# Shared gate rows and weight parts made by GpSimd transfers, in a ViT tower kernel with routed experts

## The chip, the cores and the metric

One core of a Trainium2 chip runs the whole program. The metric is the device time of one execution in microseconds; lower is better. In the rows, PE is TensorE's matmuls, PEld its weight loads, DVE VectorE, ACT ScalarE, POOL GpSimd, SP SyncE.

## The reference, cut to what matters

32 images of 96x96 pixels are cut into 36 patches each; with a class token there are T = 37 tokens an image and C = 192 channels.

```python
h   = einsum('bnk,ok->bno', patches, W)              # tok; the class token is put ahead
h   = x0 = LN(h); k, v, r = x0 @ Wk, x0 @ Wv, x0 @ Wr
x1  = x0 + (sigmoid(r) * bi_wkv(decay, first, k, v)) @ Wo      # two scans over tokens
h   = (h + x1) + sigmoid(LN(x1) @ Wr_f) * (relu(LN(x1) @ Wk_f)**2 @ Wv_f)
c   = routing of LN(h): 16 experts in 4 groups, the best 4 of the best 2 groups, weights * 2.5
hs  = silu(x @ sWg + sbg) * (x @ sWu + sbu)                    # shared expert, 192 wide
he  = silu(einsum('th,ehi->tei', x, gWg) + gbg) * (... gWu + gbu)   # 16 experts, 96 wide
out = h + hs @ sWd + sbd + einsum('te,teh->th', c, he @ gWd + gbd)
```

(LN, the gains and the residual order are shortened here; the shape of the work is what matters.)

## The kernel before, in words

The 1184 tokens are cut into four groups of 6, 10, 10 and 6 images (222, 370, 370 and 222 columns). Each group g goes through a front F{g} (patches, first norm, k/v/r, scans, Wo), a middle M{g} (second norm, `up0..5` and `mix0..5`, third norm, router logits and the routing on VectorE), and 14 expert units: `G{g}:g{n}` and `v{n}` are the gate and value matmuls of unit n on TensorE, `Y{g}:e{n}` its silu on ScalarE, `S{g}:s{n}` the product on VectorE, `X{g}:x{n}` the multiplication by the token's gate, `D{g}:d{n}` the down matmul. Units 0 and 1 are the shared expert; units 2 to 13 are the 16 experts' 1536 inner rows in 12 chunks of 128 rows. As an expert has 96 rows, a chunk covers parts of two experts, and three chunks (a period) cover four.

Each engine takes its steps in the order of a list written out by hand or by a planner (`PE_ORDER`, `ACT_ORDER`, `DVE_ORDER`, `POOL_ORDER`; L1248 to L1311). `advance` (L293) walks it; nothing is reordered at run time, so a step that waits holds up all behind it on its engine. `W:` and `L:` are steps on weights, `H:` are spins: matmuls of a constant tile that keep TensorE at work early on (L1018).

**Weights.** The matmuls that need float32 accuracy use two parts of each weight, `hi` (rounded to fp32r) and `lo` (the rest). `PIECES` (L60) are loaded by SyncE through a ring of four buffers `raw` that lies in the `gates` tile (L126 to L128). For each piece ScalarE makes `hi` by a copy (L400). For pieces before `egu0` (k, v, r, rf, up0, up1, router, sgu) VectorE subtracts to make `lo` (L610); for the six `egu` pieces TensorE does it with identity matmuls into the PSUM tile PA (L1014, L1015), in twelve halves, and ScalarE copies each half out (L409). `split` (L108) is the wait for a piece's `lo`.

**Gates.** Once group g is routed, ScalarE copies the 16 experts' gate rows out (`C{g}:cT`, L586), SyncE stores them to `c_rows` in DRAM (L329) and reads them back, each row broadcast over the partitions of its expert, by 24 transfers a group (L338): six `SPANS` for each of four periods. For g > 0 each period waits until the group before has used its gates (L335). `patches(3)`, the pixels for F3, is issued by SyncE behind the 24 transfers of group 0 (L368, L369); the stores of a finished group behind those of a later one.

**The stretch that the change moves most.** VectorE does F0's scans and products (L699 to L771), whose end is `F0:z`, then F1's, and between them the middle of group 0. GpSimd takes the inverse roots of the variances (L391), twelve in all. TensorE's front of group 1 (`F1:tr1a` on) is followed by `F1:sub0..2` (subtractions in PSUM, L1118), M0 and then the units of group 0 from `G0:g0`, which need `stack3`, VectorE's `M0:tr3a` and `M0:tr3b` (L678).

## Time and profile before

| what | value |
|---|---|
| runs before | 258.48 us median of 3 (258.15 to 259.61) |
| the profiled execution | 259.53 us, of which the span of its records is 257.6 us |
| busy in the span | PE 245.2, DVE 191.2, ACT 151.5, POOL 17.1 us |
| chain that ended last | PE 74%, DVE 9%, ACT 9%, issue 3%, DMA 2% |
| HBM read | 16.22 MB, mean 67 GB/s |

The profile is one execution. Each engine's records are listed with what ended the idle time before them; the chain is the work that ended last, followed back from the end. A busy PE includes matmuls whose end is modelled, and matmuls overlap, so the distance between the starts of two pieces of work is the better measure of their cost.

### The profile page before, as it was taken

The numbers are of one execution on the slowest core, as the hardware profiler recorded it, in microseconds if no ns is written. First come the engines' busy times: TensorE is split into PE (matmuls) and PEld (weight loads), VectorE is DVE, ScalarE is ACT, GpSimd is POOL, SyncE is SP. The second block draws the span as 40 slices with busy tenths as digits, with TensorE's granted clock in tenths as the row PEclk, the third lists the DMA queues.
The fourth block names the chain that finished last, engine by engine and source line by source line (L and its number), as shares of the span: only waits on it lengthen the run. The fifth ranks groups of instructions, "written<-read, shape, count | busy, mean of one in ns | idle before, by whom it ended". The sixth has DMA issues, their size and how long they took to land.

```text
span 257.6 us, 4492 instructions
## 1 busy us (share of the span) xinstructions
PE 245.2 (95%) x1508; PEld 222.6 (86%) x1508; DVE 191.2 (74%) x491; ACT 151.5 (59%) x312; POOL 17.1 (7%) x26
## 2 busy tenths in 40 slices
...
GB/s 154 211 191 286 212 186 119 0 3 0 0 0 6 84 111 57 0 3 0 1 3 121 187 76 4 1 3 0 54 163 158 29 3 0 1 23 109 102 29 26
DMA packets 13015, 17.49 MB, mean 68 GB/s; under 512 B 2336, under 2 KB 11074, under 8 KB 12866
## 3 DMA queue, kind: packets, MB, share of 16 engines
...
q8 instruction: 12, 0.20, 0.3%
q10 hardware_dynamic: 272, 0.11, 0.2%
...
HBM read 16.22 MB, written 0.99 MB: 67 GB/s over the span
## 4 chain that ended last, share of the span: by engine, by line
PE 74%; DVE 9%; ACT 9%; issue 3%; DMA 2%; POOL 0%; SPq 0%; DVEq 0%; POOLq 0%; ACTq 0%
PE PG L964 18%; PE PA L984 17%; PE PG L966 11%; PE PF L984 7%; PE PQ L964 4%; PE PQ L966 3%; PE PX L1001 2%; PE PF L1001 2%; ACT norm L417 2%; DMA w_tok<-in_w_tok 2%; PE PF L974 1%; PE PG L1119 1%; PE PG L1118 1%; DVE K L763 1%; PE PF L991 1%
## 5 line engine op out<-in xcount | busy, mean ns | idle before, releaser
L575 ACT ACTIVATE act<-PG,columns 128x222 f32<-128x222 f32 (+3 forms) x56 | 28.4, 507 | 59.0 <-PE PG L966 45.9
L964 PE MATMUL PG<-stack,hi_egu 128*128 128x222 f32 (+1 forms) x288 | 62.2, 324 | 0.0
L913 DVE SCALAR_TENSOR_TENSOR hid<-PG,columns,act 128x222 f32<-128x222 f32 (+1 forms) x52 | 27.3, 524 | 29.3 <-PE PG L966 26.7
L984 PE MATMUL PA<-w_ed,hid 128*124 128x192 f32 (+1 forms) x240 | 46.1, 327 | 0.6 <-DVE hid L922 0.5
L964 PEld LDWEIGHTS PG<-stack,hi_egu 128*128 128x128 f32 x288 | 45.7, 191 | 0.9 <-DVE hid L913 0.4
L966 PE MATMUL PG<-stack,lo_egu 128*128 128x222 f32 (+1 forms) x192 | 42.8, 304 | 0.0
L984 PEld LDWEIGHTS PA<-w_ed,hid 128*124 128x124 f32 (+1 forms) x240 | 38.6, 183 | 1.3 <-issue 1.3
L966 PEld LDWEIGHTS PG<-stack,lo_egu 128*128 128x128 f32 x192 | 31.8, 191 | 0.0
L391 POOL TENSOR_TENSOR rstd<-var,minus_half 112x2 f32<-112x2 f32 (+3 forms) x12 | 13.8, 1146 | 191.7 <-DVE var L657 191.7
L922 DVE TENSOR_TENSOR hid<-hid,gates 128x222 f32<-128x222 f32 (+1 forms) x48 | 21.9, 461 | 1.6 <-DMA gates<-c_rows 0.7
L984 PE MATMUL PF<-w_down,mix_hid 128*124 128x192 f32 (+1 forms) x120 | 22.8, 326 | 0.0
L984 PEld LDWEIGHTS PF<-w_down,mix_hid 128*124 128x124 f32 (+1 forms) x120 | 19.5, 183 | 0.3 <-issue 0.2
L740 DVE TENSOR_TENSOR_SCAN S<-E,S 128x333 f32<-128x333 f32 (+1 forms) x16 | 16.2, 1062 | 0.2
L964 PE MATMUL PQ<-stack,hi_up 128*128 128x222 f32 (+1 forms) x72 | 15.3, 320 | 0.0
L541 ACT ACTIVATE relu<-PQ 128x222 f32<-128x222 f32 (+1 forms) x24 | 9.9, 414 | 5.6 <-PE PQ L966 5.3
L1014 PE MATMUL PA<-gates,columns 128*128 128x512 f32 x24 | 12.5, 602 | 0.7 <-ACT lo_egu L409 0.7
L763 DVE RECIPROCAL K<-K 128x222 f32<-128x222 f32 (+3 forms) x8 | 12.2, 1531 | 0.1
L417 ACT ACTIVATE norm<-h,shift,rstd 124x192 f32<-124x192 f32 (+1 forms) x20 | 9.6, 537 | 3.9 <-DVE shift L664 3.8
L964 PEld LDWEIGHTS PQ<-stack,hi_up 128*128 128x128 f32 x72 | 11.3, 191 | 0.5 <-issue 0.5
L1021 PE MATMUL PQ<-still 128*128 128x256 f32 x36 | 10.5, 451 | 1.1 <-POOL still L385 1.1
L547 ACT ACTIVATE mix_hid<-relu 128x222 f32<-128x222 f32 (+1 forms) x24 | 10.8, 451 | 0.8
L966 PE MATMUL PQ<-stack,lo_up 128*128 128x222 f32 (+1 forms) x48 | 10.7, 304 | 0.0
...
## 6 DMA issues: line engine op xcount, KB each, us to landing
gates<-in_w_egu SPq DMA_DIRECT2D x6, 512.0 KB, 4.9
...
```

Source lines behind the costliest of these rows:

```text
L391: nc.gpsimd.tensor_tensor(small[n]["rstd"][0:G.tp, 0:cols, 0:G.tiles], small[n]["var"][0:G.tp, 0:cols, 0:G.tiles], minus_half[0:G.tp, 0:co ...
L417: last = nc.scalar.activation(norm[n][0:G.tp, t, :], x[0:G.tp, t, :], ACT.Identity, bias=small[n]["shift"][0:G.tp, col, t:t + 1], scale=sm ...
L547: nc.scalar.activation(mix_hid[:, m % 2, 0:G.n], relu[:, 0:G.n], ACT.Square).then_inc(act_square, 1)
L575: nc.scalar.activation(act[128 - gate:128, n % 2, 0:G.n], PG[0:gate, gate_bank(n), 0:G.n], ACT.Silu, bias=bias).then_inc(act_silu, 1)
L740: step(V_.tensor_tensor_scan(run(x, d), run(E1[:, d * WK:d * WK + wk], d), run(x, d), 0.0, ALU.mult, ALU.add))
L763: step(V_.reciprocal(K[:, s], K[:, s]))
L913: V_.scalar_tensor_tensor(out, PG[part, 1, 0:G.n], bias, act[part, i, 0:G.n], ALU.add, ALU.mult).then_inc(mul_done, 1)
L922: V_.tensor_tensor(out, out, gates[:, n - SCH, 0:G.n], ALU.mult).then_inc(hid_ready, 1)
L964: mm(out, w_hi[:, slot, cols], x[:, p, 0:G.n], start=(p == 0), stop=False, skip_group_check=True)
L966: last = mm(out, w_lo[:, p, cols], x[:, p, 0:G.n], start=False, stop=(p == 1), skip_group_check=True)
L984: last = mm(tile_out(P, G, t), src[:, G.ts[t]:G.ts[t] + G.tp], w, start=start and t != 1, stop=stop, skip_group_check=True)
L1014: mm(PA[:, s, 0:cols], ident32, raw[n % RING][:, s * cols:(s + 1) * cols], start=True, stop=False)
```

## The change

Two things are changed, and all four order lists are new.

Gates: the experts' rows are laid out anew (`_beside`): a period's 384 rows are arranged so that each of its three chunks has 32 rows of each of four experts. One gate tile of 128 partitions then serves three chunks. A group takes 4 transfers, each reading 4 rows of `c_rows` and repeating each over 32 partitions. There are two sets of gate tiles in turn, in the tile `ring`, and the wait is for the group two before.

Weights: rf, up0, up1, sgu and egu0 to egu5 no longer go through the ring. GpSimd issues a converting transfer from DRAM for `hi` (`W:`), ScalarE writes its negative to `lo` (`L:` in ACT_ORDER), and GpSimd issues a second transfer from DRAM which adds the weight to it (`L:` in POOL_ORDER). ScalarE's `hi` copies of these pieces, VectorE's four subtractions, TensorE's identity matmuls and ScalarE's copies of their results are gone. PA is free in that stretch, so the subtractions `F0:sub` and `F1:sub` go there, and a few waits follow.

```diff
     yield from ((m, 128, 2, cols, True) for m, cols in (("k", 256), ("v", 128), ("r", 256)))
-    yield ("rf", 128, 2, C, True)
-    yield from ((f"up{i}", 128, 2, HID // 2, True) for i in range(2))
     yield ("router", 128, 2, EXPERTS, True)
-    yield ("sgu", 128, 2, 2 * C, True)
-    yield from ((f"egu{i}", 128, 2, 512, True) for i in range(ECH // 2))
+
+
+def _cast_pieces():
+
+    yield ("rf", C)
+    yield from ((f"up{i}", HID // 2) for i in range(2))
+    yield ("sgu", 2 * C)
+    yield from ((f"egu{i}", 512) for i in range(ECH // 2))
...
-        gates = sb("gates", [128, ECH, N])
-        flat_gates = gates[:, :, :].rearrange("p c n -> p (c n)")
-        raw = [flat_gates[:, i * RING_COLS:(i + 1) * RING_COLS] for i in range(RING)]
+        ring = sb("ring", [128, RING * RING_COLS])
+        raw = [ring[:, i * RING_COLS:(i + 1) * RING_COLS] for i in range(RING)]
+        gates = [[ring[:, (i * PERIODS + j) * N:(i * PERIODS + j + 1) * N] for j in range(PERIODS)] for i in range(2)]
...
-            return PG[:, :, :].rearrange("p b c -> p (b c)") if g else (PQ, PX)[i % 2]
+            return PA[:, :, :].rearrange("p b c -> p (b c)") if g else PA[:, i % 2, :]
```

SyncE's part, then GpSimd's, ScalarE's and TensorE's:

```diff
                 if g == 0:
-                    split(sp, len(PIECES))
+                    sp.wait_ge(lo_done, len(PIECES))
                 for j in range(PERIODS):
-                    if g:
-                        sp.wait_ge(hid_ready, at(hid_ready, g - 1, 3 * (j + 1)))
-                    for chunk, a, b, e in SPANS:
-                        expert = 4 * j + e
-                        sp.dma_start(gates[a:b, 3 * j + chunk, 0:n],
-                                     A["c_rows"][g, expert:expert + 1, 0:n].broadcast_to([b - a, n])).then_inc(gates_in[j], 16)
+                    if g >= 2:
+                        sp.wait_ge(hid_ready, at(hid_ready, g - 2, 3 * (j + 1)))
+                    rows = A["c_rows"][g, BESIDE * j:BESIDE * (j + 1), None, 0:n].broadcast_to([BESIDE, 128 // BESIDE, n])
+                    sp.dma_start(gates[g % 2][j][:, 0:n], rows).then_inc(gates_in[j], 16)
...
             piece(5)
             patches(1)
-            for n in range(6, 8):
-                piece(n)
             unsplit("down")
-            for n in range(8, 10):
-                piece(n)
             unsplit("sd")
-            for n in range(10, 13):
-                piece(n)
             unsplit("ed")
-            for n in range(13, len(PIECES)):
-                piece(n)
             patches(2)
             gates_across(0)
             patches(3)
```

```diff
-            for n, g in POOL_ORDER:
-                root(n, g, 2 if n == 1 else 1)
+            def pool_roots(pool, g):
+                for n in (1, 2, 3):
+                    root(n, g, 2 if n == 1 else 1)
+                    yield f"root{n}"
+
+            def pool_casts(pool):
+                for name, _ in CAST:
+                    nc.gpsimd.dma_start(hi[name][:, :, :], A[f"w_{name}"]).then_inc(cast_in[name], 16)
+                    yield name
+
+            def pool_lows(pool):
+                for n, (name, _) in enumerate(CAST):
+                    pool.wait_ge(act_minus, n + 1)
+                    nc.gpsimd.dma_start(lo[name][:, :, :], A[f"w_{name}"], accum_op=ALU.add).then_inc(low_in[name], 16)
+                    yield name
+
+            tracks = tracks_of(pool, pool_casts, R=pool_roots)
+            advance({**tracks, "L": pool_lows(pool)}, POOL_ORDER)
```

```diff
+        def act_minus_parts(act_e):
+
+            for name, _ in CAST:
+                act_e.wait_ge(cast_in[name], 16)
+                nc.scalar.activation(lo[name][:, :, :], hi[name][:, :, :].bitcast(F32), ACT.Copy, scale=-1.0).then_inc(act_minus, 1)
+                yield name
...
-            split(pe, PIECE_AT[name] + 1)
+            if name in low_in:
+                pe.wait_ge(low_in[name], 16)
+            else:
+                pe.wait_ge(lo_done, PIECE_AT[name] + 1)
...
-
-        def pe_low_parts(pe):
-
-            pe.wait_ge(consts_done, 1)
-            for i, (name, _, slots, cols, _) in enumerate(PIECES[FIRST_EGU:]):
-                n = FIRST_EGU + i
-                for s in range(slots):
-                    k = 2 * i + s
-                    if k >= 2:
-                        pe.wait_ge(act_low, k - 1)
-                    pe.wait_ge(hi_done, n + 1)
-                    mm(PA[:, s, 0:cols], ident32, raw[n % RING][:, s * cols:(s + 1) * cols], start=True, stop=False)
-                    mm(PA[:, s, 0:cols], minus_ident[:, :], hi[name][:, s, :], start=False, stop=True).then_inc(pe_low, 1)
-                    yield f"{name}{'ab'[s]}"
```

The lists up to the first units of group 0 (the rest is rearranged in the same manner):

```diff
-POOL_ORDER = [(1, 0), (1, 1), (2, 0), (1, 2), (3, 0), (2, 1), (1, 3), (3, 1), (2, 2), (3, 2), (2, 3), (3, 3)]
+POOL_ORDER = _order(
+    "R0:root1 R1:root1 W:rf W:up0 W:up1 W:sgu W:egu0 W:egu1 W:egu2 L:rf L:up0 R0:root2 L:up1 L:sgu R2:root1 W:egu3 W:egu4",
+    "W:egu5 L:egu0 L:egu1 L:egu2 R0:root3 R1:root2 L:egu3 L:egu4 L:egu5 R3:root1 R1:root3 R2:root2 R2:root3 R3:root2",
+    "R3:root3",
+)
 PE_ORDER = _order(
-    "H:early0 H:early1 H:early2 H:early3 F0:tok0 H:early4 H:early5 H:tok H:stats0 H:stats1 H:aggr H:var H:rstd F0:tr1a",
-    "F0:tr1b F1:tok0 F1:tok1 F0:k F0:kt F0:v F0:rt F0:r H:scan0 H:scan1 H:sb0 H:sb1 H:e1 H:edge F0:sub0 F0:sub1 F0:sub2",
-    "W:egu0a W:egu0b W:egu1a F1:tr1a F1:tr1b W:egu1b W:egu2a F0:o0 F1:k F1:kt F1:v W:egu2b F1:rt F1:r M0:tr2 F2:tok0",
-    "W:egu3a F2:tok1 F1:sub0 M0:rf M0:up0 F1:sub1 M0:up1 M0:mix0 F1:sub2 M0:up2 M0:mix1 M0:up3 M0:mix2 M0:up4 M0:mix3",
-    "M0:up5 W:egu3b M0:mix4 M0:mix5 F2:tr1a W:egu4a W:egu4b F2:tr1b W:egu5a W:egu5b M0:tr3 F1:o0 M0:logits F1:o1 G0:g0",
-    "G0:g1 F2:k G0:v1 G0:g2 F2:kt G0:v2 G0:g3 F2:v D0:cT G0:v3 G0:g4 F2:rt D0:d1 M1:tr2 F2:r G0:v4 G0:g5 D0:d0 M1:rf M1:up0",
-    "D0:d2 D0:d3 M1:up1 M1:mix0 G0:v5 G0:g6 M1:up2 M1:mix1 D0:d4 M1:up3 M1:mix2 F3:tok0 G0:v6 M1:up4 M1:mix3 G0:g7 G0:v7",
...
+    "H:early0 H:early1 H:early2 H:early3 H:early4 F0:tok0 H:early5 H:tok H:stats0 H:stats1 H:aggr H:var F0:tr1a F0:tr1b",
+    "H:rstd F1:tok0 F1:tok1 F0:k F0:kt F0:v F0:rt F0:r H:scan0 H:scan1 H:sb0 H:sb1 H:e1 F0:sub0 F0:sub1 F0:sub2 F1:tr1a",
+    "F1:tr1b H:edge F1:k F1:kt F0:o0 F1:v F1:rt F1:r F2:tok0 F1:sub0 F2:tok1 F1:sub1 M0:tr2 F1:sub2 M0:rf M0:up0 M0:up1",
+    "M0:mix0 M0:up2 M0:mix1 F2:tr1a M0:up3 M0:mix2 M0:up4 M0:mix3 M0:up5 M0:mix4 F2:tr1b M0:mix5 F1:o0 F1:o1 M0:tr3 F2:k",
+    "G0:g0 M0:logits G0:g1 F2:kt G0:v1 G0:g2 F2:v G0:v2 G0:g3 F2:rt D0:cT D0:d1 G0:v3 G0:g4 M1:tr2 F2:r G0:v4 G0:g5 D0:d0",
+    "M1:rf M1:up0 D0:d2 F3:tok0 G0:v5 M1:up1 M1:mix0 D0:d3 G0:g6 M1:up2 M1:mix1 G0:v6 D0:d4 M1:up3 M1:mix2 G0:g7 D0:d5",
...
 )
 ACT_ORDER = _order(
-    "W:cls W:mask W:k W:v F0:tok0 W:r F0:ln1 Z0:x0 F0:tr1a F0:tr1b W:rf W:up0 W:up1 F0:k F0:kt F0:vt F0:kf F0:v F0:rt",
-    "W:router F1:tok0 F1:tok1 F0:r F0:exps F0:expe W:sgu W:egu0 F0:w0 F0:w1 F0:w2 W:egu1 W:egu2 L:egu0a F0:wr F1:ln1",
-    "L:egu0b L:egu1a F1:tr1a F1:tr1b L:egu1b L:egu2a W:egu3 F1:k F1:kt F1:vt F1:kf F1:v M0:ln2 F1:rt Z1:x0 F1:r F1:exps",
-    "F2:tok0 M0:tr2 F2:tok1 F1:expe F1:w0 L:egu2b M0:rf M0:mix0 W:egu4 F1:w1 M0:mix1 W:egu5 F1:w2 M0:mix2 L:egu3a M0:mix3",
-    "M0:mix4 F1:wr M0:mix5 F2:ln1 L:egu3b F2:tr1a L:egu4a L:egu4b F2:tr1b M0:ln3 M0:tr3 L:egu5a M0:logits Y0:e0 Y0:e1",
-    "L:egu5b F2:k Y0:e2 F2:kt F2:vt F2:kf Y0:e3 F2:v C0:cT M1:ln2 F2:rt Y0:e4 M1:tr2 Y0:e5 F2:r F2:exps M1:rf M1:mix0",
...
+    "W:cls W:mask W:k F0:tok0 W:v W:r F0:ln1 Z0:x0 F0:tr1a F0:tr1b F1:tok0 F1:tok1 F0:k F0:kt F0:vt F0:kf F0:v W:router",
+    "F0:rt F0:r F0:exps F0:expe F1:ln1 F0:w0 L:rf F0:w1 F0:w2 F1:tr1a F1:tr1b F0:wr L:up0 L:up1 L:sgu L:egu0 F1:k F1:kt",
+    "F1:vt F1:kf F1:v F1:rt L:egu1 F1:r L:egu2 F1:exps F1:expe F2:tok0 F1:w0 M0:ln2 Z1:x0 F2:tok1 F1:w1 M0:tr2 F1:w2 F1:wr",
+    "M0:rf M0:mix0 M0:mix1 F2:ln1 M0:mix2 M0:mix3 F2:tr1a M0:mix4 M0:mix5 F2:tr1b L:egu3 M0:ln3 M0:tr3 Y0:e0 F2:k M0:logits",
+    "Y0:e1 F2:kt F2:vt F2:kf Y0:e2 F2:v M1:ln2 Y0:e3 F2:rt C0:cT Z2:x0 Y0:e4 M1:tr2 F2:r Y0:e5 F2:exps M1:rf M1:mix0",
+    "F2:expe F2:w0 F2:w1 F2:w2 F2:wr M1:mix1 F3:tok0 Y0:e6 M1:mix2 L:egu4 L:egu5 M1:mix3 Y0:e7 Y0:e8 F3:ln1 F3:tr1a M1:mix4",
```

```diff
 DVE_ORDER = _order(
-    "W:cls W:mask W:k F0:stats1 F0:aggr1 F0:var1 W:v F0:ln1 W:r F0:tr1a F0:tr1b W:rf W:up0 W:up1 F0:scan0 F0:scan1 F0:sb",
-    "F0:e1 F1:stats1 F0:edge W:router F0:top0 F0:top1 F0:sa F1:aggr1 F0:ab00 F0:ab01 F0:ab10 F0:ab11 F1:var1 F0:weigh0",
-    "F0:weigh1 F0:own F0:sum F1:ln1 F0:sum2 W:sgu F0:den F0:recip0 F0:recip1 F0:z F1:tr1a F1:tr1b F0:x10 F0:x1 M0:stats2",
-    "M0:aggr2 M0:var2 F1:scan0 M0:ln2 F1:scan1 F1:sb F1:e1 F1:edge F1:top0 F1:top1 F1:sa M0:tr2a M0:tr2b F2:stats1 F1:ab00",
-    "F1:ab01 F1:ab10 F1:ab11 F2:aggr1 F1:weigh0 F1:weigh1 F1:own F2:var1 F1:sum F1:sum2 F2:ln1 F1:den F1:recip0 M0:gated",
-    "M0:h1 M0:stats3 M0:aggr3 M0:var3 F1:recip1 M0:ln3 F1:z F2:tr1a F2:tr1b M0:tr3a M0:tr3b F1:x10 M0:high M0:logits",
-    "M0:score M0:scores F1:x11 M0:pairs F1:x1 M0:sides S0:s0 M0:groups M0:apart M0:ahead M1:stats2 M0:rank S0:s1 M0:among",
...
+    "W:cls W:mask F0:stats1 F0:aggr1 F0:var1 F0:ln1 W:k W:v F0:tr1a W:r F0:tr1b F1:stats1 F1:aggr1 F1:var1 F0:scan0",
+    "F0:scan1 F0:sb F0:e1 F0:edge F0:top0 F0:top1 F1:ln1 F0:sa F0:ab00 F0:ab01 F0:ab10 F0:ab11 F0:weigh0 F0:weigh1 F0:own",
+    "F1:tr1a F0:sum W:router F0:sum2 F1:tr1b F0:den F0:recip0 F0:recip1 F0:z F1:scan0 F1:scan1 F1:sb F1:e1 F1:edge F0:x10",
+    "F1:top0 F0:x1 F1:top1 M0:stats2 M0:aggr2 M0:var2 F1:sa M0:ln2 F1:ab00 F1:ab01 F1:ab10 F1:ab11 M0:tr2a F2:stats1",
+    "M0:tr2b F2:aggr1 F2:var1 F1:weigh0 F1:weigh1 F1:own F2:ln1 F1:sum F1:sum2 F1:den F1:recip0 F1:recip1 F1:z M0:gated",
+    "M0:h1 M0:stats3 M0:aggr3 M0:var3 F1:x10 M0:ln3 F2:tr1a F2:tr1b F1:x11 F1:x1 M0:tr3a M0:tr3b M1:stats2 M1:aggr2 M0:high",
+    "M0:logits S0:s0 M0:score M0:scores M1:var2 M0:pairs M0:sides M0:groups M0:apart M0:ahead M0:rank M0:among S0:s1",
...
 )
```

## Rows read from the trace of the kernel before

**Rows 1.** table of stretches: stretch, then busy us of each engine, PEclk, DMA share, GB/s

```profile
28.00:36.80 8.80, 6.74 (x23) 3.13 (x21) 8.65 (x17) 8.49 (x16) 1.86 (x1) 1.00 0.39 136
...
62.70:74.00 11.30, 10.69 (x52) 7.23 (x51) 10.34 (x22) 8.51 (x18) 0.69 (x1) 1.00 0.00 0
...
104.00:240.00 136.00, 135.85 (x905) 134.27 (x905) 95.13 (x282) 64.17 (x136) 5.26 (x6) 1.00 0.16 46
```

**Rows 2.** chain that ended last, before 37 us: start us, us, what

```profile
17.55 1.83 DVE lo_up L610 x2
```

**Rows 3.** timeline of VectorE to 82 us: start us, us, engine, line, operation, [idle before]

```profile
22.44 0.87 DVE L647 BATCH_NORM_STATS2 stats<-h 124x6 f32<-124x192 f32 x3
...
32.15 0.95 DVE L610 TENSOR_TENSOR lo_sgu<-gates,hi_sgu 128x768 fp32r<-128x768 f32 x1
...
36.42 0.27 DVE L771 TENSOR_TENSOR Zt<-K,E 64x111 f32<-64x111 f32 x1
...
38.45 0.55 DVE L777 TENSOR_TENSOR x<-x,PF 112x384 f32<-112x384 f32 x1 [0.62 <-PE PF L1001]
...
40.73 1.31 DVE L699 TENSOR_TENSOR_SCAN mx<-dec,K 128x555 f32<-128x555 f32 x1
42.57 0.16 DVE L664 SCALAR_TENSOR_TENSOR shift<-mv,rstd 112x2 f32<-112x2 f32 x1 [0.52 <-POOL rstd L391]
...
62.92 0.74 DVE L759 SCALAR_TENSOR_TENSOR K<-R,E 128x555 f32<-128x555 f32 x1 [0.45 <-ACT R L503]
...
71.97 0.81 DVE L678 TENSOR_TENSOR stack<-PF,stack 128x222 fp32r<-128x222 f32 x2
72.81 0.56 DVE L777 TENSOR_TENSOR x<-x,PX 124x384 f32<-124x384 f32 x1
...
75.10 0.75 DVE L781 TENSOR_TENSOR base<-h,x 124x576 f32<-124x576 f32 x1
```

**Rows 4.** timeline of TensorE to 82 us

```profile
28.02 1.02 PE L1014 MATMUL PA<-gates,columns 128*128 128x512 f32 x2
...
29.11 1.02 PE L1014 MATMUL PA<-gates,columns 128*128 128x512 f32 x2
...
74.04 0.62 PE L964 MATMUL PG<-stack,hi_sgu 128*128 128x222 f32 x3
```

**Rows 5.** timeline of TensorE, 82 to 118 us

```profile
88.01 0.57 PE L974 MATMUL PF<-hi_rf,stack 128*124 128x192 f32 x3 [0.47 <-DVE stack L678]
...
100.16 1.53 PE L1001 MATMUL PX<-w_tok,pat 128*112 128x192 f32 x8 [0.67 <-issue]
```

**Rows 6.** timeline of ScalarE to 82 us

```profile
18.78 0.26 ACT L457 ACTIVATE K<-PF 64x111 f32<-64x111 f32 x1
...
28.56 2.00 ACT L400 ACTIVATE hi_egu<-gates 128x1024 fp32r<-128x1024 f32 x2
```

**Rows 7.** timeline of ScalarE, 82 to 118 us

```profile
102.65 1.28 ACT L503 ACT_TABLE_LOAD   x1
```

**Rows 8.** timeline of GpSimd to 82 us

```profile
28.60 1.86 POOL L391 TENSOR_TENSOR rstd<-var,minus_half 124x6 f32<-124x6 f32 x1 [16.29 <-DVE var L657]
...
59.91 2.32 POOL L391 TENSOR_TENSOR rstd<-var,minus_half 124x6 f32<-124x6 f32 x1 [17.38 <-DVE var L657]
```

**Rows 9.** DMA issues of the page: KB each, median us to landing

```profile
gates<-in_w_egu SPq DMA_DIRECT2D x6, 512.0 KB, 4.9
```

**Rows 10.** timeline of SyncE's issuing, after 37 us

```profile
83.85 13.14 SPq L338 DMA_DIRECT2D gates<-c_rows  x24
97.03 0.59 SPq L324 DMA_DIRECT2D pat<-in_patches  x1
```

**Rows 11.** DMA queues in the stretch 80 to 100 us

```profile
q1 hardware_dynamic: 2224, 1.61, 34.8%
```

**Rows 12.** table of stretches, the kernel's last microseconds

```profile
252.00:255.50 3.50, 1.75 (x10) 1.16 (x9) 1.39 (x3) 0.00 (x0) 0.00 (x0) 1.00 0.00 0
255.50:256.00 0.50, 0.00 (x0) 0.00 (x0) 0.00 (x0) 0.00 (x0) 0.00 (x0) 0.53 0.48 137
```

More of the change, by code:

```diff
@@ L74 @@
 PIECE_AT = {p[0]: n for n, p in enumerate(PIECES)}
+CAST = list(_cast_pieces())
 RING, RING_COLS = 4, 2 * 512
 PERIODS = ECH // 3
-FIRST_EGU = PIECE_AT["egu0"]
-SPANS = ((0, 0, 96, 0), (0, 96, 128, 1), (1, 0, 64, 1), (1, 64, 128, 2), (2, 0, 32, 2), (2, 32, 128, 3))
+BESIDE = 128 // 32
 DOWNS = [1, 0, *range(2, UNITS)]
@@ L106, in at @@
             return g * per_group[s] + n
-        def split(engine, pieces):
-            own = min(pieces, FIRST_EGU)
-            engine.wait_ge(lo_done, own)
-            if pieces > own:
-                engine.wait_ge(act_low, 2 * (pieces - own))
         def since(engine, s, g):
```

42 lines of the change are left out of this document (21 added, 21 removed), and 71 rows, old and new, of tables (ACT_ORDER, DVE_ORDER, PE_ORDER).

## The prediction, made before the changed kernel had run

> **What bounds the kernel now.** I read the table of stretches first. From 104 to 240 us TensorE is busy for 135.85 of 136 us [rows 1]: whatever happens there on other engines is hidden, and only less work on TensorE, or an earlier start of that stretch, moves the end. Before 74 us it is otherwise. From 28 to 36.8 us VectorE is busy for 8.65 of 8.8 us and TensorE for 6.74, and from 62.7 to 74 us VectorE for 10.34 of 11.3. The chain there runs through VectorE: the subtractions for `lo_up` stand in it right ahead of F0's scans [rows 2], and at the other end it is `M0:tr3a/b`, over at 71.97 + 0.81 = 72.8 us [rows 3], that lets group 0's units begin at 74.04 [rows 4]. So the kernel is a chain on VectorE of some 55 us, then 180 us of TensorE's work, then a tail of about 3 us that nothing here touches. What the change is worth is how much sooner `G0:g0` starts, with how much of TensorE's work then still to do, and which waits behind it go.
>
> **The change, part by part.**
>
> *TensorE's identity matmuls.* Twelve halves go. Two of them start 29.11 - 28.02 = 1.09 us apart [rows 4], so 13.1 us of TensorE's time goes. That isn't 13 us off the end: all twelve lie before `G0:g0`, five of them (5.5 us) in 28 to 36.8 us and five more in 62.7 to 74 us, where VectorE sets the pace. By themselves I cost them at nothing; their cover is the chain on VectorE, and they are worth something only as far as that gets shorter.
>
> *VectorE's chain, from F0's first scan to `M0:tr3b`.* Before, it runs from the end of the row of `lo_up`, 17.55 + 1.83 = 19.4, to 72.8: 53.4 us. (a) The start: `lo_rf` and `lo_up` are gone ahead of it, and ScalarE no longer has their copies to make. But the scan also needs K's tail, which ScalarE has copied by 18.78 + 0.26 = 19.0 [rows 6], and ScalarE gets F1's tok copies ahead of it. So the gain is nearer to 0.4 than to the 1.83 of the row, and can't be less than 0. I take 0.4. (b) `lo_sgu` goes: 0.95 [rows 3]. (c) F1's statistics (0.87, [rows 3]) with their aggregates and variances (five small ones at about 0.1 apart) move ahead of the scan into a time in which VectorE waits for F0's K: 1.3. (d) Waits: `x10` waits 0.62 for TensorE, now it stands behind F1's scans; the denominator waits 0.45 for ScalarE's R [rows 3], which has less to do: 1.07 gone. M0's root is now waited for behind one shorter step: 0.2 more. (e) `F1:x10`, `x11` and `x1` move in ahead of `M0:tr3a`: 0.56, about 0.35, 0.75 [rows 3], 1.66 more. Sum: -0.4 - 0.95 - 1.3 - 1.07 + 0.2 + 1.66 = -1.9. Adding up the new list step by step from the same trace instead I come to -1.1. I take -1.5: `M0:tr3b` ends at 71.3.
>
> *TensorE at the start of the units.* `G0:g0` came 74.04 - 72.8 = 1.2 us behind `tr3b`, as the logits and `F1:o1` stood between. They don't any more; it follows in about 0.1, at 71.4, 2.6 us earlier. `F2:k` is already done then (5 matmuls on 370 columns, 0.85) and the logits (0.6) are still to do: 0.25 more. TensorE is ahead by 2.9.
>
> *Gates and SyncE.* Before, group 0's 24 issues hold SyncE for 13.14 us, and patches(3) is issued at 97.03 behind them; F3's tok matmuls then start at 100.16 after a wait of 0.67 [rows 5, 10], which fits a landing some 3 us after the issue. With 4 issues at 13.14/24 = 0.55 us patches(3) goes out some 11 us sooner, so this wait goes even though F3:tok0 is moved up: 0.67. Nothing else hangs on the gates: a third of the bytes and a sixth of the issues go, in stretches where TensorE hides them. VectorE's products with the gates stay as many and as long.
>
> The last sentence needs the transfers to be quick enough. In 80 to 100 us 2224 packets took 34.8% of 16 engines for 20 us, 0.05 us each [rows 11]. A new transfer has 128: 0.4 us if all sixteen take part. The Trainium skill (DMA: Bandwidth & Descriptors, section on why a DMA increments its semaphore by 16) says that the number of engines must divide the slowest dimension of both sides; the source's is 4 here, so four engines would take it. By that an estimate is 32 packets each, 1.6 us a transfer at the rows' rate and 6.4 for a group. No run here shows it yet, and both sums come out the same, since three chunks of TensorE's work, at two unit steps of 0.56 and a down step of 0.65 each, last 5.3 us.
>
> *Other waits from 74 to 104 us.* TensorE waits 0.47 at 88.01 for M1's stack [rows 5] and twice about 0.3 near 76 and 80. ScalarE loses two loads of its table (1.28 each, the first of them in [rows 7]), as `F2:wr` is moved ahead of the silus, and gets the negatives of egu4 and egu5 in that place: two at 2.00/2 = 1.0 [rows 6]. Equal, to half a microsecond. The bounds are all of these waits gone (1.1) and one new wait of the kind (0.7 longer); I take 0.5.
>
> *ScalarE and the converting transfers.* Ten negatives (about 1.0 for egu, 0.75 for up and sgu) take the place of ten copies of the same size; the twelve copies of halves, 0.59 each, go. New is that in its list `L:rf`, `up0`, `up1`, `sgu`, `egu0` stand ahead of `F1:k`, and each waits for its transfer. GpSimd issues them behind F1's root, which took 1.86 us before [rows 8], so from about 20.2 if F1's variances are there at 18.3, behind `F0:tr1b`. With p for one issue, egu0 lands at 20.2 + 5p + 4.9 [rows 9]. F1:k must be copied soon after 33.5 for F1's scans to start behind `F0:z`. No row shows a GpSimd issue: SyncE's 0.55 is the near one, the longest root, 2.32, bounds it from above. I take 1.0: landing at 30, negative done by 33, no delay. At 2.32 it lands at 36.7 and F1's scans start 2.8 us late. The second transfers have over 10 us of slack before their first use. GpSimd's list puts six issues ahead of M0's third root; they start at about 56.6 and the root is wanted at 68.1, so that from p = 1.9 on it is late.
> The Trainium skill (DMA: Bandwidth & Descriptors, Anatomy of one DMA) has 2.0 us + bytes/436 GB/s for such a transfer: 3.2 us for egu0, an estimate; the row's 4.9 is used.
>
> *TensorE's clock.* Before, TensorE thins out at the end, with 1.75 us of work from 252 to 255.5, and just after this the granted clock reads 0.53, down from 2.4 GHz to 1.2 [rows 12]. Without the identity matmuls the stretch from 62.7 to 74 has 10.69 - 5.45 = 5.2 us of work in 11.3, and 28 to 36.8 has 6.74 - 5.45 = 1.3, with F1:k and kt moved in 3.0 in 8.8 [rows 1]. Both become as thin as they were not before. If the clock falls there, pieces take twice as long for a few microseconds. Around F1's front most of that is under VectorE; at `F2:k` and the first units up to 2 us are not. The bounds are 0 and 3; I take 1.0.
>
> Sum: 2.9 + 0.67 + 0.5 - 1.0 = 3.1 us. The profiled execution was 259.53 (span 257.6 and 1.93 around it), so it would be 256.4; it lies 1.05 above the median. I forecast 258.48 - 3.1 = 255.4.
>
> **The rivals.**
>
> A. *The clock holds.* The spins and the moved work are enough; then nothing is given back: 254.4, or 252.5 if the start gains the upper bound of 1.8 as well. For it: from 28 to 36.8 us TensorE had no work for 2 us in all before, too, and the clock read 1.00 [rows 1].
>
> B. *GpSimd is the new bound (slower).* If p is 2.32 or more, F1's scans are 2.8 us late and M0's third root another 6 x 2.32 - 11.5 = 2.4. Then 255.4 + 5.2 = 260.6. It decides from p = 1.5 (first place) and 1.9 (second), where it is still near 255.4. For it: GpSimd's roots took 1.86 and 2.32 us with VectorE fully at work [rows 8]. Against it: issuing reads nothing wide. An adding transfer that crawls ends the same way.
> The Trainium skill (SBUF — State Buffer, the box on the DVE that blocks DMA) says that GpSimd can't write descriptors while VectorE runs a copy or tensor_scalar in its two-port mode, but can beside tensor_tensor. Nearly all of VectorE's work here is of the second kind, so the rule speaks for a small p.
>
> C. *The clock falls in both stretches and group 0's units start cold:* three microseconds given back, not one: 257.4 to 258. The gain is then within what can't be told from no change.
>
> D. *Gates come late.* If one engine carried a transfer, its 128 packets would take 6.4 us for 5.3 us of work, 1.1 lost in each period, at least 16 periods: 255.4 + 17 = 272. Four engines don't do this.
>
> E. *The lists have a stall that the rows don't show,* such as `L:egu5` ahead of F3's root on GpSimd: 1 to 2 us, 256.4 to 257.4.
>
> **How the numbers follow.** Forecast 255.4 with a chance of 0.43, A 0.20, B 0.13, C 0.10, D 0.02, E 0.12. The forecast's own range is 254 to 257. 252.5 takes in A; 259 leaves out the strong form of B and D. Half a percent, 1.3 us, is about what a measurement of this kernel can tell from no change. Faster than 257.2: forecast, A, nearly all of E, a third of C: 0.74. Within: the rest of C and E, the weak form of B: 0.14. Slower than 259.8: B's strong form and D: 0.12.
>
> **What would show it.** Right: `F0:z` near 36 us and F1's first scan right behind it rather than at 40.73 [rows 3]; `G0:g0` near 71.4; no wait ahead of F3:tok0; gate transfers' issues under 3 us a group; TensorE still solid from 104 on. Wrong: ScalarE waiting on a converting transfer ahead of F1:k; GpSimd's issues over 1.5 us; VectorE waiting for a root; TensorE's matmuls at twice their length around 70 us; a wait of VectorE for gate rows.

## The result, and the profile after

The changed kernel takes 261.58 us (median of 20 runs, 259.2 to 266.03). The kernel before, run beside it, takes 259.53 (20 runs: nineteen from 258.15 to 260.65 and a stray one of 405.29). Six of the changed kernel's runs, the profiled one among them, were in a slower state (263.2 us and up), so the comparison goes by the other fourteen, whose median is 260.29. The ratio of these is 1.0056, 95% interval 1.0034 to 1.0077: slower by half a percent, where 1.2% faster had been forecast. The profiled execution of after took 265.33 us with a span of 263.4. No other execution of this kernel has a trace, so its rows show a longer execution than most, and what they lose is more than what the median lost. Over all twenty runs the time follows TensorE's mean granted clock: 259.2 us at 0.993, 259.38 to 260.0 at 0.979 to 0.98, 263.74 to 266.03 at 0.960 to 0.966.

The page of the kernel after: TensorE's granted clock in 40 slices, then the issues of the new transfers (KB each, median us to landing).

```profile
PEclk9999868899989977999999999999999999999999
...
hi_egu<-in_w_egu POOLq DMA_DIRECT2D x6, 512.0 KB, 6.6
lo_egu<-in_w_egu POOLq DMA_DIRECT2D x6, 512.0 KB, 8.6
```

A slice is 6.6 us. The clock falls in slices 5 to 8, 12, and 15 and 16; in windows of 2 us the first of these are two falls, one at 30 to 38 us and one at 44 to 48. The table of stretches of after, in the stretches of [rows 1], with 88 to 104 us added (stretch, busy us of PE, PEld, DVE, ACT, POOL, then PEclk, DMA share, GB/s):

```profile
28.00:36.80 8.80, 4.91 (x15) 4.43 (x16) 7.58 (x14) 6.47 (x13) 0.85 (x1) 0.65 0.63 133
62.70:74.00 11.30, 8.22 (x43) 6.84 (x42) 10.48 (x24) 7.01 (x13) 1.56 (x2) 0.89 0.87 184
88.00:104.00 16.00, 12.87 (x65) 12.03 (x65) 9.53 (x14) 10.32 (x18) 0.00 (x0) 0.79 0.15 36
104.00:240.00 136.00, 135.77 (x892) 133.37 (x891) 97.61 (x282) 64.89 (x137) 8.91 (x8) 1.00 0.10 26
```

From 104 us TensorE is as solid as before, so the loss lies ahead of that. The third line is new in kind: where before TensorE was without work for 0.7 us of these 16 (15.32 busy), it is now for 3.1, and works at less than the full clock in what is left. The timelines of after say why, first SyncE's issuing, then TensorE:

```profile
82.49 0.33 SPq L329 DMA_DIRECT2D c_rows<-hid_s  x1
84.95 2.27 SPq L337 DMA_DIRECT2D ring<-c_rows  x4
87.26 0.70 SPq L324 DMA_DIRECT2D pat<-in_patches  x1
```

```profile
31.58 1.30 PE L972 MATMUL PG<-stack,hi_k 128*128 128x370 f32 x3 [3.93 <-DVE stack L683]
...
44.13 1.94 PE L1110 MATMUL PA<-mx,columns 128*128 128x512 f32 x2 [1.99 <-DVE top L724]
...
73.41 0.81 PE L972 MATMUL PG<-stack,hi_sgu 128*128 128x222 f32 x3
...
94.16 1.62 PE L1009 MATMUL PX<-w_tok,pat 128*112 128x192 f32 x8 [3.13 <-issue]
...
99.09 2.12 PE L992 MATMUL PF<-w_down,mix_hid 128*124 128x192 f32 x6
```

The four gate issues take 2.27 us instead of 13.14, and the pixels go out at 87.26 instead of 97.03 [rows 10]. Yet `F3:tok0` waits 3.13 us for them, where it waited 0.67 [rows 5], and the pixels take 6.8 us to land where they took 3.0. VectorE then waits 6.18 us in its turn, for work that TensorE did late, as its timeline of after shows at 102.49. What the DMA engines did meanwhile stands in the table of after (the last but one number is the busy share of the sixteen):

```profile
87.50:88.50 1.00, 0.87 (x8) 0.87 (x9) 0.81 (x2) 0.98 (x2) 0.00 (x0) 1.00 0.26 68
88.50:89.50 1.00, 1.00 (x11) 1.00 (x10) 0.90 (x2) 0.99 (x2) 0.00 (x0) 1.00 0.65 80
89.50:90.50 1.00, 1.00 (x7) 1.00 (x7) 0.96 (x3) 1.00 (x3) 0.00 (x0) 1.00 0.74 188
90.50:91.50 1.00, 0.52 (x4) 0.21 (x2) 1.00 (x2) 0.97 (x4) 0.00 (x0) 1.00 0.44 137
91.50:92.50 1.00, 0.00 (x0) 0.00 (x0) 1.00 (x3) 1.00 (x3) 0.00 (x0) 1.00 0.27 86
```

A quarter of the engines (0.26) is busy while the gates move alone, some three quarters while the pixels move too, and from 91.5 us on a quarter again (0.27). So most of the pixels have moved by 91.5, and what TensorE still waits for is their share on the engines that carry the gates. In VectorE's timeline stands the second surprise, a wait ahead of F1's first scan:

```profile
18.28 1.59 DVE L704 TENSOR_TENSOR_SCAN mx<-dec,K 128x333 f32<-128x333 f32 x2 [0.51 <-ACT K L462]
...
36.31 2.52 DVE L704 TENSOR_TENSOR_SCAN mx<-dec,K 128x555 f32<-128x555 f32 x2 [1.07 <-ACT K L462]
...
102.49 0.45 DVE L918 SCALAR_TENSOR_TENSOR hid<-PG,columns,act 128x222 f32<-128x222 f32 x1 [6.18 <-PE PA L992]
```

F1's scans begin at 36.31 instead of 40.73 [rows 3], so VectorE's chain is 4.4 us ahead there; but `G0:g0` is at 73.41 instead of 74.04 [rows 4], not at 71.4. That `x3` of `hi_sgu` takes 0.81 us there, where it took 0.62 [rows 4].

### The profile page after: what moved, and what is told of

Same layout as the page of the kernel before. It is cut to its first block, busy times and chain, and to the rows that moved or that the text cites. A ratio compares the mean times of both kernels' runs of the same rounds, so it can differ in the third digit from the quotient of the medians.

```text
span 263.4 us, 4317 instructions
## 1 busy us (share of the span) xinstructions
PE 241.0 (91%) x1472; PEld 222.8 (85%) x1472; DVE 188.7 (72%) x487; ACT 142.9 (54%) x298; POOL 32.8 (12%) x46
## 4 chain that ended last, share of the span: by engine, by line
PE 67%; DVE 16%; ACT 5%; issue 5%; DMA 4%; POOL 1%; SPq 0%; DVEq 0%; POOLq 0%; ACTq 0%
PE PG L972 16%; PE PA L992 16%; PE PG L974 11%; PE PF L992 5%; PE PQ L972 2%; PE PX L1009 2%; DVE K L768 2%; DMA ring<-c_rows 2%; DMA w_tok<-in_w_tok 2%; PE PQ L974 2%; DVE mx L704 2%; PE PF L999 2%; DVE S L750 1%; DVE S L745 1%; PE PX L972 1%
## 5 line engine op out<-in xcount | busy, mean ns | idle before, releaser
L972 PE MATMUL PG<-stack,hi_egu 128*128 128x222 f32 (+1 forms) x288 | 63.0, 327 | 0.2
L992 PE MATMUL PA<-w_ed,hid 128*124 128x192 f32 (+1 forms) x240 | 47.2, 330 | 0.6 <-DVE hid L927 0.5
L992 PEld LDWEIGHTS PA<-w_ed,hid 128*124 128x124 f32 (+1 forms) x240 | 39.3, 185 | 1.0 <-issue 0.8
L381 POOL TENSOR_TENSOR rstd<-var,minus_half 112x2 f32<-112x2 f32 (+3 forms) x12 | 15.5, 1289 | 146.3 <-DVE var L662 146.3
L992 PE MATMUL PF<-w_down,mix_hid 128*124 128x192 f32 (+1 forms) x120 | 24.0, 336 | 0.0
L927 DVE TENSOR_TENSOR hid<-hid,ring 128x222 f32<-128x222 f32 (+1 forms) x48 | 21.9, 462 | 2.1 <-DMA ring<-c_rows 1.3
L992 PEld LDWEIGHTS PF<-w_down,mix_hid 128*124 128x124 f32 (+1 forms) x120 | 20.4, 190 | 0.1
L972 PE MATMUL PQ<-stack,hi_up 128*128 128x222 f32 (+1 forms) x72 | 16.3, 336 | 0.9 <-ACT relu L546 0.9
L1015 PE MATMUL PQ<-still 128*128 128x256 f32 x36 | 11.3, 461 | 1.1 <-POOL still L375 1.1
L1015 PEld LDWEIGHTS PQ<-still 128*128 128x128 f32 x36 | 7.7, 229 | 2.8 <-POOL still L375 1.1
## 6 DMA issues: line engine op xcount, KB each, us to landing
ring<-c_rows SPq DMA_DIRECT2D x8, 185.0 KB
```

What stands on the lines that cost most here:

```text
L381: nc.gpsimd.tensor_tensor(small[n]["rstd"][0:G.tp, 0:cols, 0:G.tiles], small[n]["var"][0:G.tp, 0:cols, 0:G.tiles], minus_half[0:G.tp, 0:co ...
L927: V_.tensor_tensor(out, out, gates[g % 2][(n - SCH) // 3][:, 0:G.n], ALU.mult).then_inc(hid_ready, 1)
L972: mm(out, w_hi[:, slot, cols], x[:, p, 0:G.n], start=(p == 0), stop=False, skip_group_check=True)
L992: last = mm(tile_out(P, G, t), src[:, G.ts[t]:G.ts[t] + G.tp], w, start=start and t != 1, stop=stop, skip_group_check=True)
L1015: mm(PQ[:, 0:256], still[:, 0:128], still[:, :], start=True, stop=True, skip_group_check=True)
```

## The experiments

The theory after the first look: four losses. (1) The pixels queue behind gate transfers that few DMA engines carry. (2) The clock falls in TensorE's gaps. (3) F1's K waits for its only buffer. (4) Something in the new lists. The rival for each is that the loss is hidden or that another one takes its place. Every experiment ran beside the kernel before; its median was 259.24 us beside e1 to e4, 258.86 beside e5 to e8, and 259.34 beside e9 and e10. The kernel after did not run beside them, so a difference from its 260.29 us is one across two measurements; the ratios to before, given with it, are the safer scale.

### e1: pixels first

```diff
             patches(2)
-            gates_across(0)
             patches(3)
+            gates_across(0)
```

> The changed kernel, with SyncE's patches(3) issued ahead of gates_across(0) instead of behind it; nothing else. In the changed kernel F3:tok0 waited 3.13 us for pixels that took 6.8 us to land, and TensorE's clock then read 0.50 from about 92 to 101 us, over some 9 us of work. If the wait and the clock that follows it are what ate the gain: the wait is 0, the clock stays at 1.00 after 76 us, and the time falls by 3.1 plus 2 to 4, to 254 to 256.5 us. If the loss lies in the front (converting transfers, GpSimd), the wait goes but the time stays within 1 us of the changed kernel's, as another wait takes its place.

Measured: 258.67 us (257.55 to 259.75), ratio to before 0.9995 (0.9965 to 1.0024) where after has 1.0056: 1.6 us less than after. The stretch 88 to 104 of e1, and the start of its `F3:tok0`, with no wait in the row:

```profile
88.00:104.00 16.00, 16.00 (x110) 15.66 (x111) 15.44 (x27) 14.54 (x25) 3.05 (x3) 1.00 0.19 41
```

```profile
91.22 1.46 PE L1009 MATMUL PX<-w_tok,pat 128*112 128x192 f32 x8
```

TensorE has no gap left and the clock holds there: the last fall was a consequence of the wait. That the wait and this fall are on the path is shown. In the medians they are 1.6 us, about a third of the miss of 4.6 us (1.8%). I had expected 5 to 7 us because I started from the profiled execution, and between the profiled executions it is 5.6 us (spans 263.4 and 257.8); most executions of after were shorter than the profiled one. The earlier falls of the clock stayed (0.68 at 28 to 36.8 us, 0.92 at 62.7 to 74).

### e2: the same gate tiles, filled row by row

```diff
-                    rows = A["c_rows"][g, BESIDE * j:BESIDE * (j + 1), None, 0:n].broadcast_to([BESIDE, 128 // BESIDE, n])
-                    sp.dma_start(gates[g % 2][j][:, 0:n], rows).then_inc(gates_in[j], 16)
+                    for e in range(BESIDE):
+                        part = slice(e * 128 // BESIDE, (e + 1) * 128 // BESIDE)
+                        row = A["c_rows"][g, BESIDE * j + e:BESIDE * j + e + 1, 0:n].broadcast_to([128 // BESIDE, n])
+                        sp.dma_start(gates[g % 2][j][part, 0:n], row).then_inc(gates_in[j], 16)
```

> The changed kernel, with 16 gate transfers a group, one expert's row over 32 partitions each, instead of 4 transfers of four rows; same bytes and tiles, patches(3) still behind them. If a transfer whose source has 4 rows runs on few DMA engines only, and the pixels queue behind it on those engines: the gates of group 0 now move in under 3 us of transfer time, patches(3) is issued 16 x 0.55 = 9 us after the first instead of 2.3, so about 94, and lands 3 to 3.5 us later, at 97: F3:tok0 waits longer than in the changed kernel, 5 to 6 us, and the time rises by 1 to 3 us. If the number of engines isn't the cause, the pixels' own landing time stays near 6.8 us.

Measured: 263.67 us (six runs, 262.62 to 264.4), ratio 1.0195 (1.0156 to 1.0234), 3.4 us more than after. SyncE's issuing and TensorE's wait in e2:

```profile
85.00 7.28 SPq L339 DMA_DIRECT2D ring<-c_rows  x16
92.33 0.55 SPq L324 DMA_DIRECT2D pat<-in_patches  x1
```

```profile
95.24 2.87 PE L1011 MATMUL PX<-w_tok,pat 128*112 128x192 f32 x8 [4.41 <-issue]
```

95.24 - 92.33 = 2.9 us from issue to use: with the same bytes in another form the pixels land in their old time, and the wait is longer (4.41 us, a little under the 5 to 6 expected) because 16 issues hold SyncE for 7.28 us. This alone doesn't separate two causes: the issues are spread over more time than the 6 us in which four engines moved these bytes (e5 below), so that no backlog could form whichever engines carried them. That few engines are the cause rests on the table of after above and that of e5, where the share is a quarter. Both forms delay pixels that stand behind them.

### e3: TensorE's gaps filled

Seventeen more steps with the constant tile (`H:fill`), 34 matmuls in the trace, their results unused: eight ahead of `F1:k`, four ahead of `F1:sub0`, two each ahead of `F1:o0` and `F1:o1`, one ahead of `M0:tr3`.

```diff
-    "F1:tr1b H:edge F1:k F1:kt F0:o0 ...
+    "F1:tr1b H:edge H:fill0 H:fill1 ... H:fill7 F1:k F1:kt F0:o0 ...
```

> The changed kernel, with 17 more spins of TensorE (256 columns, about 0.43 us each at the full clock) in its gaps before group 0's units: 8 ahead of F1:k, 4 ahead of F1:sub0, 2 ahead of F1:o0, 2 ahead of F1:o1, 1 ahead of M0:tr3. Theory of the clock: it stays at 1.00 until the wait for the pixels, G0:g0 starts 1 to 2 us sooner (near 72) and the time falls by 1 to 2.5 us, with less spread between executions. Rival, that the clock's falls are covered by VectorE's chain: less than 0.7 us.

Measured: 258.44 us (257.94 to 263.41; eight of twelve runs below 258.7, four from 261.14 up, so the spread didn't shrink as expected), ratio 1.001 (0.9974 to 1.0047), 1.9 us less than after. The stretches and the rows of TensorE in e3 that answer to those of after:

```profile
28.00:36.80 8.80, 6.55 (x34) 5.58 (x34) 7.58 (x14) 6.49 (x13) 0.86 (x1) 1.00 0.54 115
62.70:74.00 11.30, 10.36 (x62) 8.49 (x61) 10.16 (x32) 7.50 (x14) 0.71 (x1) 1.00 0.72 142
```

```profile
31.26 0.78 PE L972 MATMUL PG<-stack,hi_k 128*128 128x370 f32 x3 [0.47 <-DVE stack L683]
...
71.50 0.59 PE L972 MATMUL PG<-stack,hi_sgu 128*128 128x222 f32 x3 [0.34 <-DVE stack L683]
...
90.40 1.52 PE L1009 MATMUL PX<-w_tok,pat 128*112 128x192 f32 x8 [1.92 <-issue]
```

The gap of 3.93 us ahead of F1's k is full, its matmuls take 0.78 us instead of 1.30, and `G0:g0` comes at 71.50, 1.9 us sooner, of which 0.3 lies ahead of F0's scan, where no fill was added. So the clock's falls cost 1.6 us up to there, and they weren't under VectorE's chain: F1's k, v, r and o matmuls feed VectorE.

### e4: the gate half alone, on the kernel before

The weights and the lists stay as they were; only the layout of the experts' rows, the gate tiles and their 4 transfers change.

> The kernel before with the gate half of the change alone: rows laid out so that three chunks share a gate tile, 4 transfers a group, two sets of tiles; weights and all lists as before. F3:tok0 is late in the list there, at about 100 us, so the pixels (issued at about 86 instead of 97, landing by 93) are in time and its wait of 0.67 us goes: 0.5 to 1 us faster than before. If gates on few engines delay VectorE's products by themselves: slower by more than 1 us, with VectorE waiting for the gate rows in every group.

Measured: 258.43 us (257.48 to 258.83), ratio 0.9978 (0.9952 to 1.0004), which can't be told from no change. With the old lists `F3:tok0` comes later, at 99.51, the pixels have landed, and the wait is gone. The pixels took 6.0 us to land here, so the same gate transfers are harmless only because the tok step stands late.

### e5: pixels first and gaps filled (e1 + e3)

> The kernel after with both of the edits that each gained alone: the third pixels go out ahead of the first gate rows, and 17 matmuls without use fill TensorE's gaps in the fronts. Theory 1 (the pixels' wait with the clock's fall behind it, and the clock's falls at 28 to 37 and 62 to 74 us, are two separate losses): the gains add. With fills alone the span was 256.5 us with a wait for pixels of 1.92 us at 90.4; without that wait the span is 254.6 us, so the time is some 256 to 256.5 us, G0:g0 at about 71.5 us, and the clock 0.98 or more throughout. Theory 2 (the two edits gain the same microseconds, since later TensorE waits for VectorE anyway): no less than 258 us, the same as either alone.

Measured: 256.39 us (255.99 to 258.33), ratio 0.9914 (0.9883 to 0.9945); span 254.2, clock 0.999. The gains add: e3 to e5 is 2.0 us for a wait of 1.92, e1 to e5 is 2.3 us, and after to e5 3.9 us where the two edits alone have 1.6 and 1.9. The table of e5 also shows the gate transfers alone on the engines, as only they run from 84 to 88 us:

```profile
84.00:85.00 1.00, 0.20 (x2) 0.00 (x0) 0.94 (x5) 0.95 (x3) 0.00 (x0) 1.00 0.26 80
85.00:86.00 1.00, 1.00 (x9) 1.00 (x10) 1.00 (x3) 0.98 (x2) 0.00 (x0) 1.00 0.27 83
86.00:87.00 1.00, 1.00 (x11) 1.00 (x10) 0.97 (x3) 0.99 (x2) 0.00 (x0) 1.00 0.27 91
87.00:88.00 1.00, 1.00 (x8) 1.00 (x7) 1.00 (x2) 1.00 (x3) 0.00 (x0) 1.00 0.28 94
```

The DMA share is 0.26 to 0.28 of sixteen engines, steadily: four engines and a little. In 80 to 104 us the hardware queue, which carries hardly anything else there, has this row in e5:

```profile
q1 hardware_dynamic: 560, 0.47, 6.3%
```

0.063 x 24 us x 16 = 24.2 engine-microseconds (one engine busy for a microsecond each), a little of it for the store of the rows; over four engines 6.0 us. This is the rule of the Trainium skill (DMA: Bandwidth & Descriptors, "Why a DMA increments its semaphore by 16"), by which the number of engines divides the slowest dimension of both sides: the rows agree, with four. The section also says that a hardware queue takes the lowest-numbered engines, so that transfers of this shape share the same four. The steady share agrees: the four transfers are issued 0.58 us apart and each has 1.5 us of work for four engines, so that on different engines they would have overlapped and shown more than 0.28. No view names the engines one by one, so their number is shown and which they are is not.

### e6: the kernel before with the pixels first

> The kernel before with only the third pixels issued ahead of the first gate rows. Theory 1 (the 0.67 us in which F3:tok0 waits for pixels is on the path that sets the end): 0.7 us sooner, 258.0 to 258.6 us where the kernel before gives 259.2, and F3:tok0 with no wait for pixels. Theory 2 (VectorE or the clock sets the time there): within 0.3 us of the kernel before.

Measured: 258.63 us (257.04 to 261.75), ratio 0.9978 (0.9947 to 1.0008). `F3:tok0` has no wait. The interval takes in no change, so alone it decides nothing, but see the table below. The profiled execution was its longest, with a fall of the clock in its first 33 us and `G0:g0` at 77.47; only what comes behind `G0:g0` is read from it.

### e7: the kernel before with the fifth early fill sooner

```diff
-    "H:early0 H:early1 H:early2 H:early3 F0:tok0 H:early4 H:early5 ...
+    "H:early0 H:early1 H:early2 H:early3 H:early4 F0:tok0 H:early5 ...
```

> The kernel before with one step of the list moved: the fifth early fill (two matmuls) ahead of F0:tok0 instead of behind it. Theory 1 (it is what let F0:tok0 run at the full clock in the kernel after, and so gave the front its first 1.0 us): F0:tok0's matmuls take about 1.9 us instead of 2.9, F0's scan0 starts at 18.3 instead of 19.3 us, and G0:g0 comes 1 us sooner (about 73.0 instead of 74.0); the time falls by 0.5 to 1 us. Theory 2 (the 1.0 us comes from the new order of GpSimd's transfers or of the first loads): scan0 stays at 19.3 and the time stays.

Measured: 258.65 us (257.4 to 260.24), ratio 0.9989 (0.9962 to 1.0017). In the profile `F0:tok0`'s eight matmuls take 1.55 us instead of 2.90, F0's scan starts at 18.64 instead of 19.29, and `G0:g0` is at 73.42 instead of 74.04, but the time isn't measurably lower. The profiles of other kernels speak against the list as the only cause: e6, with the old order, also has 1.55, and e9, with the new one, 2.90. So the first microsecond of the kernel after, whose own eight take 1.92, may be how TensorE's clock rose in that execution. It stays open.

### e8: K in two buffers, on the kernel of e5

```diff
-        K, V, R = (sb(n, [128, WK]) for n in ("K", "V", "R"))
+        KS, V, R = [sb(f"K{i}", [128, WK]) for i in range(2)], sb("V", [128, WK]), sb("R", [128, WK])
...
-            since(act_e, z_ready, g)
             act_e.wait_ge(pe_kvr, at(pe_kvr, g, 1))
...
+            since(act_e, z_ready, g)
             tails(V, upper, upper)
```

> The kernel with both edits (pixels first, 17 fills), and K in two buffers by turns, so that ScalarE's copy of F1's k no longer waits for VectorE's last reading of F0's K (it waited 2.23 us at 35 us, and VectorE 1.07 us for it at the head of F1's scans). Theory 1 (that buffer is what holds F1's scans once the front runs 1 us sooner): VectorE's wait ahead of scan0 of F1 goes, G0:g0 comes about 1 us sooner (70.5 us) and the time is 0.5 to 1 us below that of the same kernel with one K. Theory 2 (TensorE's order holds F1's k, with fills ahead of it): the wait passes to TensorE and the time stays within 0.3 us.

Measured: 255.65 us (six runs, 255.54 to 257.85), ratio 0.9896 (0.9846 to 0.9946), the fastest kernel of this study and faster than before and after. F1's k as ScalarE copies it, in after and then in e8, and e8's scan:

```profile
35.27 0.48 ACT L467 ACTIVATE K<-PG 128x370 f32<-128x370 f32 x1 [2.23 <-DVE Zt L776]
```

```profile
33.06 0.48 ACT L466 ACTIVATE K<-PG 128x370 f32<-128x370 f32 x1
```

```profile
35.24 2.52 DVE L704 TENSOR_TENSOR_SCAN mx<-dec,K 128x555 f32<-128x555 f32 x2
```

VectorE's wait of 1.07 us is gone, and from F0's scan to `G0:g0` it is 1.05 us shorter than in e5. The medians differ by 0.74 us; the intervals of e5 and e8 overlap, so the step's size in the time isn't settled, its place is.

### e9: what is left without the weights half

The kernel of e4 with the pixels first and the fifth early fill sooner.

> The kernel before with the gate half of the change alone, the third pixels ahead of the first gate rows, and the fifth early fill ahead of F0:tok0: all that gained in the kernel after except the weights by GpSimd's transfers and the lists. Beside the kernel after with pixels first and fills (256.39 us, span 254.2, G0:g0 at 71.4 us) it tells what the weights and lists are worth once nothing waits for pixels and the clock holds in both. Theory 1 (my sum: VectorE's share of the weights' parts, off its chain up to M0:tr3, is worth some 2 us and reaches the end): G0:g0 at about 73.4 us and 258.0 to 258.4 us. Theory 2 (later TensorE waits for VectorE anyway and the lead is given back): 256.4 to 257 us, the same as with the new weights.

Measured: 257.23 us (256.92 to 258.84), ratio 0.9933 (0.9913 to 0.9953). It lies between the theories, and `G0:g0` is at 74.62, not at 73.4. By the ratios the weights half with its lists and fills is worth 0.2% more (e5, 0.9914), or 0.4% with two K (e8, 0.9896), 0.5 and 1.0 us; the intervals overlap, so that it gains anything isn't shown. e9 is also 1.2 us below e4, though the two intervals of the table below are the same in both traces; the rest may lie ahead of F0's scan, where the fill was moved, but no trace shows it, as the profiled execution was e9's longest, 258.84. It stays open.

### e10: e5 with the gates row by row

> The kernel after with pixels first and 17 fills, but each gate transfer of four rows made of four of one row over 32 partitions (16 a group). Beside the same kernel with the transfers of four rows (256.39 us): Theory 1 (once the pixels go out first, nothing that TensorE waits for stands behind the gates, so their form costs nothing): 256.1 to 256.7 us, though SP issues for 7.3 us instead of 2.3. Theory 2 (VectorE's first product with the gates waits for them, or SP's longer issuing holds the hidden states' way out): 0.5 us or more slower, with VectorE's waits at hid<-hid,ring.

Measured: 256.14 us (four runs, 255.79 to 256.34), ratio 0.9861 (0.9809 to 0.9913). With the pixels ahead, the form of the gate transfers costs nothing that can be seen, although SyncE issues for 7.30 us. Rows of four weren't bad in themselves; what stood behind them was.

## Why the prediction was wrong, step by step

Two intervals from the profiled executions keep the steps apart, whatever the first microseconds were: from F0's first scan to `G0:g0` (the chain on VectorE), and from `G0:g0` to the end of the span (TensorE's work). Each is a difference of starts read from the timelines.

| kernel | F0 scan | G0:g0 | scan to G0:g0 | G0:g0 to span end |
|---|---|---|---|---|
| before | 19.29 | 74.04 | 54.75 | 183.6 |
| predicted | 19.0 | 71.4 | 52.4 | 182.1, + 1.0 for the clock |
| after | 18.28 | 73.41 | 55.13 | 190.0 |
| e1 pixels first | 18.58 | 73.62 | 55.04 | 184.2 |
| e2 gates by row | 18.18 | 73.38 | 55.20 | 189.0 |
| e3 fills | 17.97 | 71.50 | 53.53 | 185.0 |
| e4 gates alone | 19.46 | 74.22 | 54.76 | 182.3 |
| e5 pixels, fills | 17.85 | 71.41 | 53.56 | 182.8 |
| e6 before, pixels first | 21.73 | 77.47 | 55.74 | 182.3 |
| e7 before, fill sooner | 18.64 | 73.42 | 54.78 | 183.5 |
| e8 and two K | 18.26 | 70.77 | 52.51 | 183.1 |
| e9 old weights | 19.86 | 74.62 | 54.76 | 182.3 |
| e10 e5, gates by row | 18.29 | 71.83 | 53.54 | 182.6 |

*Gates and SyncE: the step that failed.* I wrote that patches(3) goes out some 11 us sooner, "so this wait goes even though F3:tok0 is moved up", and that four engines or sixteen made no difference to the sum. From `G0:g0` the pixels' issue moved from 23.0 to 13.9 us, 9.1 sooner, but `F3:tok0` moved from 25.5 (its start less its wait) to 17.6, 7.8 sooner; that would still have done with a landing of 3 us. The landing took 6.8. I had worked out 6.4 us of four busy engines for a group and charged it to VectorE's products alone, which hardly waited, as I said: 0.26 us at 88.60. I did not ask what else uses these engines: the pixels are spread over all sixteen (a share of 0.74 at 90 us), and they have landed only when the share behind the gates has (0.27 from 91.5 us on). In place of a gain of 0.67 stood a wait of 3.1, and a stretch at the lower clock behind it. Both go in e1, which is worth 1.6 us in the medians, and 2.0 once the clock holds elsewhere (e3 to e5). Rival D looked at the same queue, but for one engine and for the gates themselves.

*TensorE's clock: right mechanism, size wrong.* The two thin stretches were named, and the clock fell in both: 0.65 and 0.89 against 1.00. A third fall, at 44 to 48 us behind the gap of 1.99 us, was not named. I took 1.0 us with bounds 0 and 3, as most of the first fall would be under VectorE. It wasn't. With the fills the time falls by 1.9 us in after and by 2.3 with the pixels first (e1 to e5). Rival C, three given back for the clock instead of one, is the nearest to this and got 0.10. The prediction looked at how much work a stretch has left; the gaps in after's rows ahead of the falls (3.93 us at 31.58, 1.99 at 44.13) were not worked out.

*VectorE's chain: right, once two things are out of its way.* The forecast for scan to `G0:g0` was 52.4 us; e8 has 52.51. That it is met to 0.1 us is partly luck, as the prediction had two sums for the chain, -1.9 and -1.1, and took the middle. In after it was 55.13. Of the 2.6 us between, the clock has 1.6 (e3: 53.53) and K's single buffer 1.05 (e8 against e5). That wait stood in the code before, but there F1's k came to ScalarE at 39.27 in the timeline of before, behind `F0:z` [rows 3]; the change moved it ahead. I looked for what ScalarE's new list puts in front of `F1:k`, not for what `F1:k` itself waits for.

*The start.* I took 0.4 and the profile has 1.0, of which e6, e7 and e9 leave open how much is the change's.

*`G0:g0`'s place.* Right: it follows `M0:tr3b` at once, at 71.4 as forecast, in e5 (71.41) and e3 (71.50). Not in after.

*GpSimd: right.* I took 1.0 us for an issue, with bounds 0.55 and 2.32, and no delay of F1's k by it; the k waits for VectorE (e8), not for an issue. GpSimd's timeline in after:

```profile
17.84 1.33 POOL L381 TENSOR_TENSOR rstd<-var,minus_half 124x6 f32<-124x6 f32 x1 [6.66 <-DVE var L662]
...
21.46 1.60 POOL L391 DMA_DIRECT2D hi_egu<-in_w_egu  x3
25.67 0.90 POOL L397 DMA_DIRECT2D lo_rf<-in_w_rf  x1 [2.61 <-ACT lo_rf L414]
```

1.60/3 = 0.53 us for a converting transfer, just under my lower bound, 0.9 for one that adds. Rival B falls. (Rival A's 252.5 takes 1.83 for the start off on top of the 0.4 that the sum has already; it should have been 253.0.)

*Other waits from 74 to 104 us, with the quarter microsecond of `F2:k`.* I took a gain of 0.75 from them. With neither gates nor pixels in the way, the old lists give 182.3 us from `G0:g0` to the end three times (e4, e6, e9), the new ones 182.8, 183.1 and 182.6 (e5, e8, e10). So that term is a loss of 0.3 to 0.8 instead, part of which stands in the rows: M1's stack, which TensorE waited 0.47 for [rows 5], takes 0.8 in e5 and 0.91 in after. The same column prices the old wait for pixels: 183.6 - 182.3 = 1.3 us, twice the 0.67 that its row shows.

The account for the median stays rougher. The falls of the clock and the wait together (e5 against after) are 3.9 us. e8, with both cured and K doubled, is 3.2 us faster than the kernel before beside it, and 3.1 was forecast for the change. That agreement is luck in part: the forecast paid 1.0 for the clock, which e8 doesn't pay (its clock is 1.000), and counted on 0.75 from the other waits, which e8 doesn't get.
